# Routed attention: the mask moves into VectorE's maxima, the normalisation to GpSimd, the output copies to VectorE

## The chip, the cores and the metric

The kernel runs on one core of a Trainium2 chip. The metric is the time of one execution in microseconds on the device; the times quoted are medians of several executions. The core has five engines that run their own instruction queues and meet only at semaphores: TensorE (matmul, PE in the profile; its weight loads have their own row, PEld), VectorE (DVE), ScalarE (ACT), GpSimd (POOL) and SyncE (SP, here only for DMA issues). Matmul results land in PSUM, eight banks of 512 float32 columns by 128 partitions. VectorE and ScalarE read PSUM; GpSimd in this kernel works on SBUF only.

## What is computed

Two transformer layers over 2048 tokens of width 512. The change touches only the last block, a routed ("mixture of depths") layer: 256 of the 2048 tokens are chosen by a score, and pass through attention with 16 query heads and 8 key heads of width 128 and through a gated MLP. Its attention is

```
q = (h @ wq + bq).reshape(S, N_HEADS, HEAD_DIM)          # S = 256, 16 heads of 128
...
att = jnp.einsum('shd,thd->hst', q, kk) / np.sqrt(HEAD_DIM)
causal = jnp.tril(jnp.ones((S, S), bool))
att = jnp.where(causal[None], att, jnp.finfo(att.dtype).min)
att = jax.nn.softmax(att, axis=-1)
attn_out = jnp.einsum('hst,thd->shd', att, v).reshape(S, N_HEADS * HEAD_DIM) @ wo
```

The output of all blocks is a tensor of 1 x 2048 x 512 in float32.

## The kernel before, in words

`stage_routed` (line 2451) runs after everything else. It projects queries, keys and values (lines 2539 to 2550), does the 16 heads of attention, then the output projection (L83, called from line 2596), the norm, the gated MLP and the scatter into the output.

The 256 tokens are two tiles of 128. By causality the first tile of queries (m = 0) sees 128 keys and the second (m = 1) sees 256, so the scores of a head are 128 x 384 numbers in one PSUM bank: columns 0 to 127 for m = 0 and 128 to 383 for m = 1. Three banks (`SB`) are used in turn. For each head:

- TensorE, `scores(h)`, line 2553: for each m one float32 score matmul (L2558; in the profile each float32 matmul counts twice), and behind it a bfloat16 matmul of the identity with `G.lower` (L2560), which adds -1e30 above the diagonal into the same bank.
- VectorE, `maxima(h)`, line 2688: two reductions out of PSUM with negation (L2692), then one scaling of both results (L2696, tile `nm`).
- ScalarE, `probabilities(h)`, line 2624: two exponentials out of PSUM into the SBUF tile `pr`, with the row sums (L2629).
- VectorE, `normalised(h)`, line 2698: the reciprocals of both sums (L2700) and two multiplications of `pr` in place, 128 and 256 columns (L2703).
- TensorE, `spread(h)`, line 2564: three transposes of `pr` into PSUM (L2568). ScalarE, `spread(h)`: one copy of the 384 columns to `pt` (L2636).
- TensorE, `attend(h)`, line 2571: two products with the values (L2577, L2578). ScalarE, `output(h)`, line 2638: a copy of 128 x 256 out of PSUM to `oT` (L2640; the tile is called `bias` in the profile).

The order on each engine is written out by hand. TensorE: scores 0, scores 1, then for each h scores(h+2), spread(h), attend(h-1). VectorE: maxima 0, maxima 1, then for each h normalised(h), maxima(h+2). ScalarE: probabilities 0 and 1, then for each h spread(h), probabilities(h+2), output(h-1). GpSimd has no work in the heads: it does one multiplication for each unit of queries and keys (L2511) before them, and the scatter (L2519) at the very end. `pr`, `nm`, `ssum` and `rsum` have three buffers each, `pt` and the PSUM banks of the transposes and of the values two.

The other attention of this layer (`stage_attend1`) is not touched, but uses, on VectorE at L2134, the instruction that the change brings here, with its one-column memset (L2132), and on GpSimd an in-place select (L2036). `SB[h % 3]` is the bank of head h, and the semaphores `s_mm`, `nm_done`, `p_done`, `pn_done`, `pt_mm`, `pt_done`, `av_mm`, `o_done` count these steps in the order given.

Of the kernel before, what the change touches and what calls it, by code (L numbers as in the profile page):

```python
# [17 lines left out]
P = 128  # L18
F32 = mybir.dt.float32
F32R = mybir.dt.float32r  # L20
BF16 = mybir.dt.bfloat16
U32 = mybir.dt.uint32
I32 = mybir.dt.int32
ALU = mybir.AluOpType
ACT = mybir.ActivationFunctionType
AX = mybir.AxisListType.X
# [11 lines left out]
NEG = -1e30  # L38
# [6 lines left out]
SEL = T // 8  # L45
NS = SEL // P
NHQ, NHK, HDF = 16, 8, 128
# [469 lines left out]
def wait(eng, sem, value):  # L517

    if not isinstance(value, int) or value > 0:
        eng.wait_ge(sem, value)  # L520
# [1930 lines left out]
def stage_routed(nc, G, I, R, out):  # L2451


    names = ("qk_mm", "qb", "t1", "y", "yt_mm", "yt", "v_mm", "v", "link")
    qk_mm, qb_done, t1_done, y_done, yt_mm, yt_done, v_mm, v_done, link = (G.sem("ro_" + n) for n in names)
    b_in, hT_done = R.b_in, R.hT_done
    names = ("s_mm", "nm", "p", "pn", "pt_mm", "pt", "av_mm", "o", "wo_mm", "x1", "gu_mm", "sig", "m", "dn_mm", "delta", "gate")
    s_mm, nm_done, p_done, pn_done, pt_mm, pt_done, av_mm, o_done, wo_mm, x1_done, gu_mm, sig_done, m_done, dn_mm, delta_done, gate_done = (
        G.sem("ro_" + n) for n in names)
    wo_in, wgu_in, wd_in, added = (G.sem("ro_" + n) for n in ("wo_in", "wgu_in", "wd_in", "added"))  # L2460
    FQ, FK = NHQ * HDF, NHK * HDF
# [3 lines left out]
    scale = 1.0 / float(np.sqrt(HDF))  # L2465
    with ExitStack() as stack:
        M = Memory(nc, stack, "ro_")
# [7 lines left out]
        oT = bias[:, :].rearrange("p (h n) -> p h n", h=NHQ)  # L2475
        qT = M.sb("qT", [P, NHQ, SEL])
        kT, v = M.sb("kT", [P, NHK, SEL]), M.sb("v", [P, NS, FK])
        xs, cs, sc, hn, hT = R.xs, R.cs, R.sc, R.hn, R.hT
        x1 = M.sb("x1", [P, NS, D])
        qb, t1, y = (M.sb(n, [P, 2, BANK]) for n in ("qb", "t1", "y"))  # L2480
        nm, ssum, rsum = (M.sb(n, [P, 3, NS]) for n in ("nm", "ssum", "rsum"))
        SB = (0, 1, 6)
        pr, pt = M.sb("pr", [P, 3, 3 * P]), M.sb("pt", [P, 2, 3 * P])
        sig = M.sb("sig", [P, 2, SEL])
        gate = M.sb("gate", [P, NS])
        block = stack.enter_context(nc.Block())


# [17 lines left out]
        @block.gpsimd  # L2506
        def _(pool):
            for n, (w, off, u, m, dst) in enumerate(units):
                pool.wait_ge(qb_done, n + 1)
                wait(pool, y_done, n - 1)  # L2510
                pool.tensor_tensor(t1[:, n % 2, :].rearrange("p (h d) -> p h d", d=HDF),  # L2511
                                   qb[:, n % 2, :].rearrange("p (h d) -> p h d", d=HDF),
                                   cs[0][:, m, :].unsqueeze(1).to_broadcast([P, HB, HDF]), ALU.mult).then_inc(t1_done, 1)
            for k in range(2):
                pool.wait_ge(R.out_stored[k], 16 * NT // 2)
            for m in range(NS):
                pool.wait_ge(delta_done, m + 1)
                where = bass.IndirectOffsetOnAxis(G.idx[:, m:m + 1], 0)
                pool.indirect_dma_start(out, where, hn[:, m, :], None, compute_op=ALU.add).then_inc(added, 16)  # L2519
                pool.wait_ge(added, 16 * (m + 1))  # L2520

        @block.tensor
        def _(pe):
# [27 lines left out]


            def scores(h):
                wait(pe, p_done, NS * (h - 2))
                bank = G.ps[SB[h % 3]]
                for m in range(NS):
                    out = bank[:, m * P:(2 * m + 1) * P]
                    pe.matmul(out, qT[:, h, m * P:(m + 1) * P], kT[:, h * NHK // NHQ, 0:(m + 1) * P],  # L2558
                              start=m == 0, stop=False, skip_group_check=True)
                    last = pe.matmul(bank[:, 2 * m * P:(2 * m + 1) * P], G.identb[:, :], G.lower[:, :],  # L2560
                                     start=False, stop=True, skip_group_check=True)
                last.then_inc(s_mm, 1)

            def spread(h):
# [17 lines left out]
            pe.wait_ge(qb_done, len(units))  # L2582
            pe.wait_ge(v_done, len(vunits))
            scores(0)
            scores(1)
            for h in range(NHQ):
# [13 lines left out]
            for f in range(NF):  # L2600
                wait(pe, m_done, f - 1)
                for n, w in enumerate((wg, wu)):
                    last = mm32(pe, G.ps[2 + f % 2][:, n * SEL:(n + 1) * SEL],
                                [(w[:, c, f * P:(f + 1) * P], hT[:, c, :]) for c in range(NC)])
                last.then_inc(gu_mm, 1)
            pe.wait_ge(wd_in, 16)
            for m in range(NS):
                for f in range(NF):
                    pe.wait_ge(m_done, f + 1)
                    last = pe.matmul(G.ps[4 + m], qT[:, f, m * P:(m + 1) * P], wb[:, f, :], start=f == 0, stop=f == NF - 1)  # L2610
                last.then_inc(dn_mm, 1)

        @block.scalar
        def _(act):
            def rotated(n):
                w, off, u, m, dst = units[n]
                act.wait_ge(yt_mm, n + 1)
                act.activation(dst[:, u * HB:(u + 1) * HB, m * P:(m + 1) * P],
                               G.ps[2 + n % 2].rearrange("p (h n) -> p h n", h=HB), ACT.Copy).then_inc(yt_done, 1)

            for n in range(len(units)):
                rotated(n)

            def probabilities(h):
                for m in range(NS):
                    act.wait_ge(nm_done, NS * h + m + 1)
                    if m == 0:
                        wait(act, pt_mm, h - 2)
                    act.activation(pr[:, h % 3, m * P:(2 * m + 1) * P], G.ps[SB[h % 3]][:, m * P:(2 * m + 1) * P], ACT.Exp,  # L2629
                                   bias=nm[:, h % 3, m:m + 1], scale=scale,  # L2630
                                   accum_out=ssum[:, h % 3, m:m + 1]).then_inc(p_done, 1)

            def spread(h):
                act.wait_ge(pt_mm, h + 1)
                wait(act, av_mm, h - 1)
                act.activation(pt[:, h % 2, :], G.ps[2 + h % 2][:, 0:3 * P], ACT.Copy).then_inc(pt_done, 1)  # L2636

            def output(h):
                act.wait_ge(av_mm, h + 1)
                act.activation(oT[:, h, :], G.ps[4 + h % 2][:, 0:SEL], ACT.Copy).then_inc(o_done, 1)  # L2640

            probabilities(0)
            probabilities(1)
            for h in range(NHQ):
                spread(h)
                if h + 2 < NHQ:
                    probabilities(h + 2)
                if h >= 1:
                    output(h - 1)
            output(NHQ - 1)  # L2650
            R.root(act, 1)
            act.activation(gate[:, :], sc[:, :], ACT.Sigmoid).then_inc(gate_done, 1)
            for f in range(NF):
                act.wait_ge(gu_mm, f + 1)
                wait(act, m_done, f - 1)
                act.activation(sig[:, f % 2, :], G.ps[2 + f % 2][:, 0:SEL], ACT.Sigmoid).then_inc(sig_done, 1)

        @block.vector
        def _(dve):
            chain = Chain(dve, link)  # L2660

            dve.wait_ge(b_in[0], 16)
            for n, (w, off, u, m, dst) in enumerate(units):
                dve.wait_ge(qk_mm, n + 1)
# [10 lines left out]
                for k in range(2):  # L2675
                    last = dve.tensor_tensor(y4[:, :, k * half:(k + 1) * half], q4[:, :, (1 - k) * half:(2 - k) * half],
                                             cs[1][:, m, k * half:(k + 1) * half].unsqueeze(1).to_broadcast([P, HB, half]),
                                             ALU.mult)
# [9 lines left out]
            def maxima(h):  # L2688
                dve.wait_ge(s_mm, h + 1)
                wait(dve, p_done, NS * (h - 2))  # L2690
                for m in range(NS):
                    dve.tensor_reduce(nm[:, h % 3, m:m + 1], G.ps[SB[h % 3]][:, m * P:(2 * m + 1) * P], AX, ALU.max, negate=True  # L2692
                                      ).then_inc(link, 1)
                    chain.n += 1
                dve.wait_ge(link, chain.n)
                dve.tensor_scalar(nm[:, h % 3, :], nm[:, h % 3, :], scale, None, ALU.mult).then_inc(nm_done, NS)  # L2696

            def normalised(h):
                dve.wait_ge(p_done, NS * (h + 1))
                chain.done(dve.reciprocal(rsum[:, h % 3, :], ssum[:, h % 3, :]))  # L2700
                for m in range(NS):
                    cols = slice(m * P, (2 * m + 1) * P)
                    last = dve.tensor_scalar(pr[:, h % 3, cols], pr[:, h % 3, cols], rsum[:, h % 3, m:m + 1], None, ALU.mult)  # L2703
                last.then_inc(pn_done, 1)

            maxima(0)
            maxima(1)
            for h in range(NHQ):
                normalised(h)
                if h + 2 < NHQ:  # L2710
                    maxima(h + 2)
            for m in range(NS):
                dve.wait_ge(wo_mm, m + 1)
                dve.tensor_tensor(x1[:, m, :], G.ps[m], xs[:, m, :], ALU.add).then_inc(x1_done, 1)
# [190 lines left out]
```

## Time and profile before

| what | value |
|---|---|
| median of 3 runs | 1667.73 us (1664.67 to 1669.33) |
| the profiled execution: time, span | 1670.91 us, 1669.2 us |
| busy over the span: PE, DVE, ACT, POOL | 1549.7, 993.7, 720.6, 463.8 us |
| granted TensorE clock, mean | 0.963 of full speed (full is 2.4 GHz, the lower level 0.50, 1.2 GHz) |
| first score matmul of the routed attention | 1508.17 us |
| first matmul of its output projection | 1540.90 us |

The span runs from the first to the last instruction of the profiled execution. Busy time of TensorE contains overlaps of matmuls in the pipeline, so a busy TensorE is not one at its peak. In a timeline a row "x2" merges neighbouring instructions of the same kind; its length is from the start of the first to the end of the last. In the chain of waits the rows follow each other without overlap, so that its lengths add up.

### The profile page before, as it was taken

What the parts mean: (1) busy time and instruction counts of PE and PEld (TensorE: products, weight loads), DVE (VectorE), ACT (ScalarE), POOL (GpSimd) and SP (SyncE); (2) the same over time, 40 slices, a digit from 0 to 9 for tenths busy, and PEclk for the clock granted to TensorE, in tenths of its full rate; (3) what the DMA queues carried; (4) which work ended last, traced back from release to release, by engine and by line L of the source; (5) the groups of instructions that cost most, each with busy time, mean ns of one, the idle gap of its engine ahead of it and who ended that gap; (6) DMA issues with size and microseconds to landing.
All of it is one profiled execution on the core that took longest, in us unless ns stands there. A gap on an engine that the chain in (4) does not pass through costs nothing. (4 is left out here: it accounts for less than half of the span.)

```text
span 1669.2 us, 23334 instructions
## 1 busy us (share of the span) xinstructions
PE 1549.7 (93%) x7008; PEld 1073.0 (64%) x7008; DVE 993.7 (60%) x2739; ACT 720.6 (43%) x1218; POOL 463.8 (28%) x686
## 2 busy tenths in 40 slices
PE   5999999999999998999789999999999987899898
PEld 4877888887667776788545555555554545547484
DVE  5453666666566545877566776656677754575121
ACT  5533656565674333233234455555555541116010
POOL 0000777776432322322201121122121141130000
PEclk9999999999999999899869999999999988999899
DMA  4002222221002224467790413422431115604200
GB/s 171 1 1 82 86 88 95 78 97 58 26 26 83 95 84 127 122 187 201 218 328 19 111 35 84 112 62 56 111 66 53 62 59 166 210 29 202 101 1 13
DMA packets 100811, 158.76 MB, mean 95 GB/s; under 512 B 12004, under 2 KB 63332, under 8 KB 93160
## 3 DMA queue, kind: packets, MB, share of 16 engines
q1 hardware_dynamic: 95432, 147.34, 28.8%
q0 software_dynamic: 1920, 5.51, 1.2%
q10 hardware_dynamic: 3360, 4.72, 0.8%
q8 instruction: 46, 0.75, 0.2%
q14 instruction: 53, 0.43, 0.1%
HBM read 114.67 MB, written 42.87 MB: 94 GB/s over the span
## 5 line engine op out<-in xcount | busy, mean ns | idle before, releaser
L2064 ACT ACTIVATE l_pt<-banks 128x1024 f32<-128x1024 f32 (+3 forms) x288 | 218.5, 811 | 165.8 <-PE banks L1942 163.7
L2134 DVE CUSTOM_DVE_ANT_0 stage<-banks,l_edges 128x384 f32<-128x384 f32 (+3 forms) x384 | 201.7, 542 | 102.6 <-issue 101.6
L1979 PE MATMUL banks<-l_pt,l_v 128*64 128x512 f32 (+3 forms) x1152 | 230.6, 522 | 2.4 <-POOL l_pt L2036 2.4
L699 POOL TENSOR_TENSOR ex_hl<-ex_h,ex_hh 128x512 fp32r<-128x512 f32 x128 | 165.4, 1298 | 81.4 <-ACT ex_hh L667 81.2
L2035 POOL TENSOR_TENSOR l_turn<-l_before 128x2 f32<-128x2 f32 x192 | 39.8, 207 | 422.7 <-ACT l_pt L2064 413.1
L2137 DVE TENSOR_REDUCE l_mx<-banks 128x1 f32<-128x384 f32 (+1 forms) x208 | 113.2, 544 | 50.3 <-PE banks L1920 49.5
L732 DVE SCALAR_TENSOR_TENSOR ex_rw<-banks,ex_wb 128x512 f32<-128x512 f32 x128 | 88.3, 690 | 79.2 <-PE banks L75 79.1
L1979 PEld LDWEIGHTS banks<-l_pt,l_v 128*64 128x64 f32 x1152 | 70.3, 140 | 95.3 <-issue 71.7
L667 ACT ACTIVATE ex_hh<-ex_h 128x512 fp32r<-128x512 f32 x128 | 80.9, 632 | 103.7 <-DVE ex_h L740 102.0
L1920 PE MATMUL banks<-k,q 96*128 96x384 f32 (+3 forms) x296 | 95.1, 414 | 18.7 <-PEq L2777 8.4
L73 PE MATMUL banks<-ex_xlh,ex_wh 128*128 128x512 f32 x256 | 101.7, 397 | 2.1 <-DVE ex_rw L732 2.1
L75 PE MATMUL banks<-ex_xlh,ex_wl 128*128 128x512 f32 x256 | 99.8, 390 | 0.0
L74 PE MATMUL banks<-ex_xll,ex_wh 128*128 128x512 f32 x256 | 99.8, 390 | 0.0
L1920 PEld LDWEIGHTS banks<-k,q 96*128 96x128 f32 x296 | 54.8, 206 | 70.0 <-issue 25.0
L1920 PE MATMUL banks<-l_k,l_q 96*128 96x384 f32 (+3 forms) x296 | 88.7, 383 | 9.2 <-DVE l_mx L2134 5.5
L1920 PEld LDWEIGHTS banks<-l_k,l_q 96*128 96x128 f32 x296 | 50.2, 191 | 62.5 <-DVE l_mx L2134 26.6
L740 DVE TENSOR_TENSOR ex_h<-banks,ex_t 128x512 f32<-128x512 f32 x128 | 88.3, 690 | 1.2 <-PE banks L75 0.7
L2036 POOL TENSOR_SCALAR_AFFINE_SELECT l_pt<-l_pt 128x256 f32<-128x256 f32 x192 | 79.8, 415 | 0.1
L661 ACT ACTIVATE ex_t<-ex_rw 128x512 f32<-128x512 f32 x128 | 79.0, 617 | 1.4 <-DVE ex_rw L732 1.4
L693 POOL TENSOR_TENSOR ex_wl<-ex_ws,ex_wh 128x768 fp32r<-128x768 f32 x16 | 29.6, 1852 | 149.6 <-ACT ex_wh L655 149.6
L1942 PE MATMUL banks<-q,k 98*128 98x512 f32 (+3 forms) x288 | 69.0, 360 | 1.5 <-ACT q L2083 1.4
L1942 PE MATMUL banks<-l_q,l_k 98*128 98x512 f32 (+3 forms) x288 | 67.5, 353 | 0.5 <-ACT l_pt L2064 0.5
(405 smaller groups left out, 3384.8 us busy)
## 6 DMA issues: line engine op xcount, KB each, us to landing
ex_wb<-gates_by_expert SPq DMA_DIRECT2D x16, 1024.0 KB, 4.7
layer_v<-qkv_vs SPq DMA_DIRECT2D x16, 512.0 KB, 4.9
l_v<-layer_v SPq DMA_DIRECT2D x8, 1024.0 KB, 16.6
layer_qk<-qkv_yh SPq DMA_DIRECT2D x31, 256.0 KB, 3.2
layer_qk<-qkv_yl SPq DMA_DIRECT2D x31, 256.0 KB, 3.6
ex_ws<-ew_in SPq DMA_DIRECT2D x16, 384.0 KB, 5.0
l_q<-layer_qk SPq DMA_DIRECT2D x12, 512.0 KB, 8.0
l_k<-layer_qk SPq DMA_DIRECT2D x12, 512.0 KB, 13.7
```

Of the source, the lines that this page charges most:

```text
L73: pe.matmul(out, ah, bh, start=start and n == 0, stop=False, **kw)
L74: pe.matmul(out, ah, bl, start=False, stop=False, **kw)
L75: last = pe.matmul(out, al, bh, start=False, stop=stop and end, **kw)
L699: pool.tensor_tensor(hl[:, k % RING, :], h[:, k % RING, :], raw(hh[:, k % RING, :]), ALU.subtract).then_inc(hl_done, 1)
L732: dve.scalar_tensor_tensor(rw[:, k % 2, :], gate[k % 2][:, :], 0.0, wb[:, par, b * TB:(b + 1) * TB], ALU.max, ALU.mult).then_inc(rw_done, 1)
L740: dve.tensor_tensor(h[:, k % RING, :], up[k % 2][:, :], tt[:, k % 2, :], ALU.mult).then_inc(h_done, 1)
L1920: pe.matmul(out, q[par][0:K3, h, qt * P:(qt + 1) * P], k[par][0:K3, h, k0 * P:k1 * P], start=True, stop=True).then_inc(a_mm, 1)
L1942: last = pe.matmul(bank[:, 0:width], k[par][0:KM, h, kt * P:(kt + 1) * P], q[par][0:KM, h, qa * P:(qz + 1) * P], start=True, stop=True)
L1979: last = pe.matmul(bank[h * 2 * HD:(h + 1) * 2 * HD, (qa - b * BT) * P:(qz + 1 - b * BT) * P], v[par][:, kt, h, :], pt[:, step_part(b, j), ...
L2064: act.activation(pt[:, step_part(b, j), :, 0:width], G.banks[:, 2 * slot:2 * slot + 2, 0:width], ACT.Exp, scale=scale).then_inc(p_done, 1)
L2134: dve.tensor_tensor_reduce(cutoff[:, n % 4, 0:width], G.ps[5 + n % MB][:, 0:width], masked, 1.0, NEG, ALU.add, ALU.max, mx[:, h, m, c:c + ...
L2137: dve.reduce_max(mx[:, h, m, c:c + 1], G.ps[5 + n % MB][:, 0:width], axis=AX).then_inc(a_red, 1)
```

## The change

Four edits, all in `stage_routed`. The bfloat16 mask matmuls go; VectorE adds a wide mask tile (zeros, then the causal triangle) and takes the maxima in one instruction, `tensor_tensor_reduce`, that writes the masked scores to `pr` in SBUF. ScalarE's exponential then works in place on `pr`, no longer out of PSUM. The two multiplications with the reciprocal sums go from VectorE to GpSimd, with a new semaphore `rsum`. The output copies go from ScalarE to VectorE, two heads late: `output(h - 2)` stands after `maxima(h + 2)` and so before `inverses(h + 1)`. The scores of head h wait for the maxima of head h-3 where they had waited for its exponentials, and the maxima of head h wait for the transposes of head h-3.

```diff
+        wide = M.sb("wide", [P, 2 * P], BF16)
+        carry = M.sb("carry", [P, 4, 1])
...
@@ gpsimd
+            for h in range(NHQ):
+                pool.wait_ge(rsum_done, h + 1)
+                for m in range(NS):
+                    cols = slice(m * P, (2 * m + 1) * P)
+                    last = pool.tensor_scalar(pr[:, h % 3, cols], pr[:, h % 3, cols], rsum[:, h % 3, m:m + 1], None, ALU.mult)
+                last.then_inc(pn_done, 1)
@@ tensor, scores(h)
-                wait(pe, p_done, NS * (h - 2))
+                wait(pe, nm_done, NS * (h - 2))
...
-                    out = bank[:, m * P:(2 * m + 1) * P]
-                    pe.matmul(out, qT[:, h, m * P:(m + 1) * P], kT[:, h * NHK // NHQ, 0:(m + 1) * P],
-                              start=m == 0, stop=False, skip_group_check=True)
-                    last = pe.matmul(bank[:, 2 * m * P:(2 * m + 1) * P], G.identb[:, :], G.lower[:, :],
-                                     start=False, stop=True, skip_group_check=True)
+                    last = pe.matmul(bank[:, m * P:(2 * m + 1) * P], qT[:, h, m * P:(m + 1) * P],
+                                     kT[:, h * NHK // NHQ, 0:(m + 1) * P], start=m == 0, stop=m == NS - 1,
+                                     skip_group_check=True)
@@ scalar, probabilities(h)
-                    if m == 0:
-                        wait(act, pt_mm, h - 2)
-                    act.activation(pr[:, h % 3, m * P:(2 * m + 1) * P], G.ps[SB[h % 3]][:, m * P:(2 * m + 1) * P], ACT.Exp,
+                    cols = slice(m * P, (2 * m + 1) * P)
+                    act.activation(pr[:, h % 3, cols], pr[:, h % 3, cols], ACT.Exp,
@@ scalar
-            def output(h):
-                act.wait_ge(av_mm, h + 1)
-                act.activation(oT[:, h, :], G.ps[4 + h % 2][:, 0:SEL], ACT.Copy).then_inc(o_done, 1)
...
-                if h >= 1:
-                    output(h - 1)
-            output(NHQ - 1)
@@ vector, at the start of the stage
+            dve.memset(wide[:, 0:P], 0.0)
+            chain.done(dve.tensor_copy(wide[:, P:2 * P], G.lower[:, :]))
@@ vector, maxima(h)
+                wait(dve, pt_mm, h - 2)
                 for m in range(NS):
-                    dve.tensor_reduce(nm[:, h % 3, m:m + 1], G.ps[SB[h % 3]][:, m * P:(2 * m + 1) * P], AX, ALU.max, negate=True
-                                      ).then_inc(link, 1)
+                    cols = slice(m * P, (2 * m + 1) * P)
+                    dve.memset(carry[:, 2 * (h % 2) + m, :], 0.0)
+                    dve.tensor_tensor_reduce(pr[:, h % 3, cols], G.ps[SB[h % 3]][:, cols], wide[:, (1 - m) * P:2 * P],
+                                             1.0, NEG, ALU.add, ALU.max, nm[:, h % 3, m:m + 1]).then_inc(link, 1)
...
-                dve.tensor_scalar(nm[:, h % 3, :], nm[:, h % 3, :], scale, None, ALU.mult).then_inc(nm_done, NS)
-
-            def normalised(h):
+                dve.tensor_scalar(nm[:, h % 3, :], nm[:, h % 3, :], -scale, None, ALU.mult).then_inc(nm_done, NS)
+
+            def inverses(h):
                 dve.wait_ge(p_done, NS * (h + 1))
-                chain.done(dve.reciprocal(rsum[:, h % 3, :], ssum[:, h % 3, :]))
-                for m in range(NS):
-                    cols = slice(m * P, (2 * m + 1) * P)
-                    last = dve.tensor_scalar(pr[:, h % 3, cols], pr[:, h % 3, cols], rsum[:, h % 3, m:m + 1], None, ALU.mult)
-                last.then_inc(pn_done, 1)
+                dve.reciprocal(rsum[:, h % 3, :], ssum[:, h % 3, :]).then_inc(rsum_done, 1)
+
+            def output(h):
+                dve.wait_ge(av_mm, h + 1)
+                dve.tensor_copy(oT[:, h, :], G.ps[4 + h % 2][:, 0:SEL]).then_inc(o_done, 1)
 
             maxima(0)
             maxima(1)
             for h in range(NHQ):
-                normalised(h)
+                inverses(h)
                 if h + 2 < NHQ:
                     maxima(h + 2)
+                if h >= 2:
+                    output(h - 2)
+            output(NHQ - 2)
+            output(NHQ - 1)
```

## Rows read from the trace of the kernel before

**Rows 1.** Busy time of each engine in the middle of the stage; then granted clock, DMA.

```profile
core 0: us, PE busy (x) PEld busy (x) DVE busy (x) ACT busy (x) POOL busy (x), PEclk, DMA share, GB/s
1514.60:1535.60 21.00, 21.00 (x152) 18.29 (x151) 15.77 (x68) 19.08 (x71) 0.00 (x0) 1.00 0.70 290
```

**Rows 2.** Chain of waits in order of time: start, length, engine, tile, line.

```profile
1508.17 0.46 PE banks L2558 x2
...
1518.27 0.22 PE banks L2558 x2
...
1518.55 0.49 PE banks L2558 x2
...
1519.09 0.34 PE banks L2568 x3
1519.43 0.43 PE banks L2577 x2
1519.86 0.22 PE banks L2578 x2
...
1540.90 27.72 PE banks L83 x64
```

**Rows 3.** Timeline of one head: start, length, engine, line, operation, tiles.

```profile
1519.92 0.39 PE L2558 MATMUL banks<-ro_kT,ro_qT 128*128 128x128 f32 x2
...
1520.94 0.62 DVE L2692 TENSOR_REDUCE ro_nm<-banks 128x1 f32<-128x128 f32 x2 [0.26 <-PE banks L2560]
...
1521.67 0.17 DVE L2696 TENSOR_SCALAR ro_nm<-ro_nm 128x2 f32<-128x2 f32 x1
1521.75 0.16 DVE L2700 RECIPROCAL ro_rsum<-ro_ssum 128x2 f32<-128x2 f32 x1
...
1521.94 0.55 DVE L2703 TENSOR_SCALAR ro_pr<-ro_pr,ro_rsum 128x128 f32<-128x128 f32 x2
...
1522.60 0.50 PE L2568 MATMUL banks<-ident,ro_pr 128*128 128x128 f32 x3
```

**Rows 4.** Timeline, TensorE: the transposes of heads 0, 1, 14 and 15.

```profile
1511.95 0.55 PE L2568 MATMUL banks<-ident,ro_pr 128*128 128x128 f32 x3 [0.97 <-DVE ro_pr L2703]
...
1513.40 0.55 PE L2568 MATMUL banks<-ident,ro_pr 128*128 128x128 f32 x3
...
1537.21 0.55 PE L2568 MATMUL banks<-ident,ro_pr 128*128 128x128 f32 x3 [0.61 <-DVE ro_pr L2703]
...
1538.29 0.55 PE L2568 MATMUL banks<-ident,ro_pr 128*128 128x128 f32 x3
```

**Rows 5.** VectorE: two timeline rows; groups by shape, busy us, mean ns, idle.

```profile
899.65 0.42 DVE L2134 CUSTOM_DVE_ANT_0 stage<-banks,l_edges 128x256 f32<-128x256 f32 x1 [1.19 <-issue]
...
900.11 0.17 DVE L2145 TENSOR_REDUCE l_nm<-l_mx 128x8 f32<-128x16 f32 x1
...
L2134 DVE CUSTOM_DVE_ANT_0 stage<-banks,l_edges 128x128 f32<-128x128 f32 x16 | 4.6, 285 | 2.0 <-issue 2.0
...
L2720 DVE TENSOR_TENSOR ro_sig<-banks,ro_sig 128x256 f32<-128x256 f32 x16 | 6.8, 425 | 45.7 <-ACT ro_sig L2656 45.7
...
L2703 DVE TENSOR_SCALAR ro_pr<-ro_pr,ro_rsum 128x256 f32<-128x256 f32 x16 | 5.6, 347 | 0.0
```

**Rows 6.** Timeline: a GpSimd instruction that waits for the VectorE instruction.

```profile
1453.75 0.69 DVE L2669 TENSOR_TENSOR ro_qb<-banks,bias 128x512 f32<-128x512 f32 x1
...
1454.52 1.51 POOL L2511 TENSOR_TENSOR ro_t<-ro_qb,routed_cos 128x512 f32<-128x512 f32 x1 [1.85 <-DVE ro_qb L2669]
```

**Rows 7.** GpSimd's groups by shape, over the whole span.

```profile
L699 POOL TENSOR_TENSOR ex_hl<-ex_h,ex_hh 128x512 fp32r<-128x512 f32 x128 | 165.4, 1298 | 81.4 <-ACT ex_hh L667 81.2
L2036 POOL TENSOR_SCALAR_AFFINE_SELECT l_pt<-l_pt 128x256 f32<-128x256 f32 x192 | 79.8, 415 | 0.1
...
L118 POOL TENSOR_SCALAR_AFFINE_SELECT ident<-ident 128x128 f32<-128x128 f32 x1 | 0.3, 285 | 0.2 <-POOL lower L116 0.2
```

**Rows 8.** Busy time by stretch again, of two others with TensorE partly idle.

```profile
1336.00:1346.00 10.00, 6.93 (x37) 3.41 (x35) 9.32 (x23) 3.89 (x7) 4.35 (x6) 1.00 0.00 0
...
1573.00:1581.00 8.00, 7.15 (x20) 5.76 (x21) 1.79 (x4) 0.80 (x2) 0.00 (x0) 0.50 1.04 392
```

More of the change, by code:

```diff
@@ L2456, in stage_routed @@
     b_in, hT_done = R.b_in, R.hT_done
-    names = ("s_mm", "nm", "p", "pn", "pt_mm", "pt", "av_mm", "o", "wo_mm", "x1", "gu_mm", "sig", "m", "dn_mm", "delta", "gate")
-    s_mm, nm_done, p_done, pn_done, pt_mm, pt_done, av_mm, o_done, wo_mm, x1_done, gu_mm, sig_done, m_done, dn_mm, delta_done, gate_done = (
+    names = ("s_mm", "nm", "p", "pn", "pt_mm", "pt", "av_mm", "o", "wo_mm", "x1", "gu_mm", "sig", "m", "dn_mm", "delta", "gate", "rsum")
+    s_mm, nm_done, p_done, pn_done, pt_mm, pt_done, av_mm, o_done, wo_mm, x1_done, gu_mm, sig_done, m_done, dn_mm, delta_done, gate_done, rsum_done = (
         G.sem("ro_" + n) for n in names)
```

## Prediction

> **What bounds the kernel now.** I looked first at the busy shares by stretch, to see whether the changed stage has one full engine. In the 21.00 us in the middle of the routed attention the matmul engine is busy all the time, ScalarE 19.08 us and VectorE 15.77 us; GpSimd has nothing there [rows 1]. By that view the stage is TensorE's, and the two matmuls taken out per head look like pure gain. The chain of waits, read next, gives TensorE's pieces for one head: scores 0.22, then 0.06 up to the next row for the first mask matmul, scores 0.49, 0.05 up to the transposes for the second mask matmul, three transposes 0.34, then 0.43 and 0.22 for the two products with the values, 1.81 in all [rows 2]. The stage runs from 1508.17 to 1540.90, 32.73 us [rows 2].
>
> The timeline shows a second bound that the busy share hides [rows 3]. The program order of VectorE is: normalise head h, maxima of head h+2, normalise head h+1. TensorE's order is: scores h+2, transposes h, values h-1, scores h+3, transposes h+1. So a loop runs through both engines. From the first score matmul of head h+2 (1519.92) to its first maximum is 1.02 us; 0.73 to the scaling; 0.08 to the reciprocal of head h+1; 0.19 to its normalisation; 0.55 for that pair, over at 1522.49. The transposes of head h+1 start at 1522.60, 0.11 later. Of that I take 0.05 for the wake-up. TensorE then does those transposes (0.38 when they were waited for) and values h (0.65) before it comes to scores h+4. The loop covers two heads: 1.02 + 0.73 + 0.08 + 0.19 + 0.55 + 0.05 + 0.38 + 0.65 = 3.65 us, 1.83 per head. The trace has 13 head periods between the transposes of 1513.40 and 1537.21: 23.81 us, 1.832 each [rows 4]. So TensorE and this loop bound the stage together, and the question is what the change does to the loop.
>
> **The change, step by step.**
>
> 1. Mask matmuls out. 32 go, two per head. TensorE loses their two pieces, 0.06 and 0.05 [rows 2], and the second score piece should shrink from 0.49 to the 0.43 that the same 256 columns take with the values [rows 2]: 0.17 per head. Bounds: 0.11 if only the mask pieces go, 0.17 if the other does too. I take 0.17, since the two 256-column products have the same work. TensorE alone would need 1.64 to 1.65 per head. The same 0.17 comes off the first term of the loop: 1.02 becomes 0.85.
>
> 2. Maxima with the mask. The new instruction is in the trace, in the other attention: 0.285 us for 128 columns and 0.42 for 256, and 0.46 from the start of the latter to the next instruction that needs its result (899.65 to 900.11), accumulator read included [rows 5]. The instructions overlap by 0.07, so the 128-column one adds 0.22: 0.68 until the scaling starts, against 0.73 now. The memset of one column ahead of each could add up to 0.06 each; I take nothing, since the instruction itself must wait for the matmuls and the first memset precedes only the first of them. Bounds 0.62 to 0.80.
>
> 3. The outputs come to VectorE. A copy of 128x256 out of PSUM now stands, in program order, between the scaling of head h+2 and the reciprocal of head h+1, so all of it is in the loop. A plain copy out of PSUM of that size isn't in the trace of this stage; a two-operand VectorE instruction over the same PSUM shape takes 0.425 [rows 5], less 0.07 of overlap 0.35. The bounds are 0.28 (the SBUF normalisation of the same shape, 0.347 [rows 5], less 0.07) and 0.42 (no overlap). On ScalarE the output copy goes away, but ScalarE is not in the loop. Its rest per head, two exponentials and the spread, was already finished in time; the gain there is nothing in the steady part. The data of these outputs was ready a head earlier (head h-2), so there is no wait for them.
>
> 4. Normalisation on GpSimd. The 0.19 from the reciprocal to the normalisation becomes a hand-over to another engine: from the end of a VectorE instruction (1453.75 + 0.69) to a GpSimd start is 0.08 [rows 6]; with the 0.16 of the reciprocal [rows 3] that is 0.24. For the work itself there is no GpSimd multiply by a scalar in the trace. The nearest rows are its one-input selects in place: 0.415 for 128x256 and 0.285 for 128x128 [rows 7], 0.70 for the pair. From above: a two-input GpSimd instruction takes 1.298 for 512 columns [rows 7], so by columns 0.65 + 0.32 = 0.97, and with a fixed start in each up to 1.13. From below: not under VectorE's own 0.55 [rows 3]. I take 0.70, because those are one-input, in place, float32, and of the same two shapes.
>
> The Trainium skill, "GPSIMD Engine Reference", section 8 (Key points), says that for elementwise work VectorE is structurally about twice as fast. The trace agrees for two inputs (1.298 on GpSimd [rows 7] against 0.69 on VectorE [rows 6], both 512 columns); for one input it does not (0.415 against VectorE's 0.347, 256 columns [rows 7, 5]), and section 4.1 of the page (Engine selection) itself calls one-input work roughly line-rate. By the first rule the time is that of rival A.
>
> 5. The rest. The score matmuls now wait for the maxima instead of the exponentials, which is earlier, and the maxima wait for transposes of a head that TensorE finished one period before; neither ends last. The one-time fill of the wide mask tile stands on VectorE before its first bias addition, which must wait for TensorE's first four 512-column matmuls anyway; nothing. The exponentials read SBUF in place of PSUM; off the loop.
>
> New loop for two heads: 0.85 + 0.68 + 0.08 + 0.35 + 0.24 + 0.70 + 0.05 + 0.38 + 0.65 = 3.98 us, 1.99 per head against 1.832. TensorE would now stand idle 0.34 of each period and wait for GpSimd at the transposes. 13 periods at +0.16 are +2.1 us.
>
> The ends go the other way. To the first head's transposes it is 3.78 now (1508.17 to 1511.95 [rows 2, 4]); of its terms the scores lose 0.17 and the maxima 0.05, the hand-over gains 0.05 and the normalisation 0.15: 3.76, -0.02. From there to the second head's it is 1.45 now; its probabilities will be ready, and TensorE has only the first head's transposes and the scores of head 3 in between, 0.35 and 0.65, 1.00: -0.45. The last two sets lie 1.08 apart now [rows 4], and become 0.38 + 0.65 = 1.03: -0.05. From the last set to the output projection it is 2.61 (1538.29 to 1540.90 [rows 2, 4]); the copy that ends it moves between engines at about its length, and the spread before it no longer queues behind an output copy on ScalarE, worth 0 to 0.2; I take 0. Together -0.5.
>
> Sum: 2.1 - 0.5 = **+1.6 us**, 0.1%. The profiled execution took 1670.91 us (span 1669.2), so its like would take 1672.5; it lies 3.2 above the median of the three runs, 1667.73, and on that median the forecast is **1669.3 us**.
>
> What a different price is worth: 0.1 us on the loop costs 0.05 per head, 0.65 over 13 periods, and with the first head and the fill about 0.15 more: 8 us for each us on the loop.
>
> **The rivals.**
>
> A. GpSimd is at half of VectorE's speed here too (the other side: slower). Place: the two GpSimd multiplications of each head, on the loop. VectorE's pair is 0.347 + 0.27 = 0.62 without its overlap [rows 3, 5], so 1.24. 0.54 more at 8 gives +4.3, so +5.9: 1673.6. It decides, with more than 5 us, from a pair of about 1.13. For it: the two-input row. Against it: the select rows [rows 7]. The rule of "GPSIMD Engine Reference" in the Trainium skill, told above, speaks for it.
>
> B. The clock falls. TensorE's idle share in the stage goes from nothing to some 17%. For it: after the wait near 1568 the granted clock was 0.50 for 8 us at 7.15 busy [rows 8]. Against it: 10 us at 6.93 busy kept 1.00 [rows 8]. At the lower level a head takes TensorE 3.3 instead of 1.99, so one stretch of 8 us serves 2.4 heads and not 4.0, 1.6 heads or about 3.2 us more, with the 1.6 of the forecast: 1672.5.
>
> C. The loop doesn't bind (faster). If the handover hides and TensorE sets the pace at 1.65, 13 periods give -2.4 and the ends -0.5: -2.9, 1664.8. For it: TensorE's busy share. Against it: with no output copy at all and everything else as above the loop is still 3.63, 1.82 per head; the GpSimd pair would have to take less than 0.38 for any gain in the steady part, which is below every bound of step 4.
>
> **How the numbers follow.** Forecast 0.60, A 0.19, B 0.11, C 0.10. A change within 0.3% (5 us) is what a measurement of this kernel can't tell from none. The forecast's own range, from the bounds of steps 1 to 4 (0.55 to 1.05 for the GpSimd pair, 0.1 either way for the others together), is -0.4 to +5. Faster by more: 0.01 from the forecast, 0.03 from C, 0.04. Slower by more: 0.04 from the forecast, 0.14 from A, 0.05 from B, 0.23. Same: 0.73. The range goes down to 1665.5, between C and the forecast, and up to 1674.3, just past A.
>
> **What would show it.** Head period, from one set of transposes to the next: 1.99; 1.65 shows C, 2.26 shows A, over 3 with the clock at 0.50 shows B. TensorE's wait ahead of the transposes should be put down to GpSimd, about 0.35 per head. VectorE: first maximum to scaling 0.68, output copy 0.42, right before each reciprocal. GpSimd: 16 pairs of 0.70. Scores: the 256-column piece 0.43. The forecast is wrong if the GpSimd pair is outside 0.5 to 1.1, or if TensorE waits for something else than GpSimd.

## The result: 9.4 us slower, where 1.6 was forecast

| | before | after |
|---|---|---|
| median of 14 runs each | 1666.62 us (1661.23 to 1670.43) | 1676.06 us (1669.63 to 1680.36) |
| ratio | | 1.006, 95% interval 1.0046 to 1.0074 |
| profiled execution: time, span | 1670.91, 1669.2 | 1676.22, 1674.5 |
| first score matmul to output projection | 1508.17 to 1540.90, 32.73 us | 1502.80 to 1546.89, 44.09 us |
| head period (between transposes) | 1.832 | 2.44, and 2.476 over the 13 of [rows 4] |

The stage, from the first score matmul of the routed attention to the output projection, got 11.4 us longer. The two profiled executions differ by 5.4 us the other way before the stage begins, in code that the change hardly touches. I take that as run to run: over all the kernels of this document, which share that code, the stage begins anywhere from 1499.81 to 1508.17. So the stage is what to compare, and its 11.4 lies inside the interval of the whole (7.7 to 12.3 us).

The busy times by stretch, in the same columns as [rows 1]: TensorE, full before, has 21.42 of 29.00 us; GpSimd has 17.79. Nothing looks full any more.

```profile
1512.00:1541.00 29.00, 21.42 (x129) 16.45 (x128) 14.55 (x108) 16.10 (x57) 17.79 (x25) 1.00 0.41 169
```

The timeline of the changed kernel, around one lap of the loop (two heads), answers [rows 3]:

```profile
1525.22 0.55 PE L2574 MATMUL banks<-ident,ro_pr 128*128 128x128 f32 x3 [1.23 <-POOL ro_pr L2520]
...
1526.26 0.82 PE L2565 MATMUL banks<-ro_kT,ro_qT 128*128 128x128 f32 x4
...
1527.13 0.29 DVE L2695 CUSTOM_DVE_ANT_0 ro_pr<-banks,ro_wide 128x128 f32<-128x128 f32 x1 [1.77 <-ACT ro_pr L2634]
...
1527.88 0.17 DVE L2699 TENSOR_SCALAR ro_nm<-ro_nm 128x2 f32<-128x2 f32 x1
...
1527.96 0.42 DVE L2707 COPY bias<-banks 128x256 f32<-128x256 f32 x1
...
1528.29 0.15 DVE L2703 RECIPROCAL ro_rsum<-ro_ssum 128x2 f32<-128x2 f32 x1
...
1528.54 1.51 POOL L2520 TENSOR_SCALAR ro_pr<-ro_pr,ro_rsum 128x128 f32<-128x128 f32 x2 [1.58 <-DVE ro_rsum L2703]
...
1530.10 0.55 PE L2574 MATMUL banks<-ident,ro_pr 128*128 128x128 f32 x3 [1.23 <-POOL ro_pr L2520]
```

Read the starts: scores to first maximum 0.87, to the scaling 0.75, to the output copy 0.08, to the reciprocal 0.33, to GpSimd 0.25, and then **1.56 to the transposes**. TensorE needs 1.04 from transposes to scores (1525.22 to 1526.26, at the start of the lap). 0.87 + 0.75 + 0.08 + 0.33 + 0.25 + 1.56 + 1.04 = 4.88 us for two heads, 2.44 each. The profile names ScalarE as releaser of the first maximum, but the exponentials that this maximum waits for belong to the head three before it and had ended over 4 us earlier. It starts 0.05 after the end of the score matmuls (1526.26 + 0.82), and the same 0.87 from their start stands in the laps before and after. GpSimd's groups in the changed kernel, in the columns of [rows 7] but from 1508 us on, so with 15 of the 16 heads:

```profile
L2520 POOL TENSOR_SCALAR ro_pr<-ro_pr,ro_rsum 128x256 f32<-128x256 f32 x15 | 13.9, 925 | 0.0
...
L2520 POOL TENSOR_SCALAR ro_pr<-ro_pr,ro_rsum 128x128 f32<-128x128 f32 x15 | 9.1, 605 | 13.5 <-DVE ro_rsum L2703 13.5
```

The rest is for the most part the clock. The third column from the end (PEclk) shows the granted clock at both ends of the stage below full speed; within these stretches, from 1508 to 1511 and from 1542 to 1545, it is 0.50:

```profile
1506.00:1509.00 3.00, 1.42 (x6) 1.38 (x7) 0.70 (x7) 1.13 (x5) 3.00 (x4) 0.79 1.02 434
1509.00:1512.00 3.00, 3.00 (x13) 2.25 (x11) 0.88 (x8) 2.16 (x9) 1.20 (x3) 0.65 1.01 429
...
1541.00:1544.00 3.00, 2.41 (x10) 1.91 (x10) 0.85 (x3) 1.30 (x5) 2.11 (x3) 0.64 0.00 0
1544.00:1547.00 3.00, 2.39 (x12) 2.00 (x11) 1.01 (x3) 1.77 (x2) 0.00 (x0) 0.79 0.00 0
```

### The profile page after: what moved, and what is told of

It reads as the page before. It is cut to its first block and busy times, and to the rows that moved or that the text cites. A ratio compares the mean times of both kernels' runs of the same rounds, so it can differ in the third digit from the quotient of the medians.

```text
span 1674.5 us, 23323 instructions
## 1 busy us (share of the span) xinstructions
PE 1547.2 (92%) x6976; PEld 1070.2 (64%) x6976; DVE 991.4 (59%) x2789; ACT 717.0 (43%) x1202; POOL 488.5 (29%) x718
```

## The experiments

All edits are against the changed kernel unless said otherwise. "Period" is read from the starts of the transposes in the middle of the stage, "stage" from the first score matmul to the output projection, in the profiled execution. The ratio is to the kernel before on the same chip. "GpSimd pair" is the length of GpSimd's two multiplications of one head, from the start of the first to the end of the second; in e12 there is only one. In the expected texts, theory S says that the loop's sum is right and only this pair was mis-sized; rival O says that the order of work on VectorE cost the time.

| run | GpSimd pair | loop sum expected | period | stage | ratio (95%) |
|---|---|---|---|---|---|
| before | none | 1.83 | 1.83 | 32.73 | |
| changed | 1.51 | (1.99) | 2.44 | 44.09 | 1.006 (1.0046 to 1.0074) |
| e1 normalisation on VectorE | none | 1.93 | 1.93 | 35.68 | 1.0008 (0.9993 to 1.0023) |
| e2 GpSimd alone, on before | 1.50 | 2.33 | 2.34 | 42.35 | 1.0044 (1.0028 to 1.0061) |
| e3 mask alone | none | 1.76 | 1.77 | 31.85 | 0.9997 (0.9981 to 1.0014) |
| e4 output copy out of the loop | 1.50 | 2.27 | 2.27 | 41.90 | 1.0059 (1.0038 to 1.008) |
| e5 constant | 1.34 | 2.04 or 2.4 | 2.35 | 42.14 | one run |
| e6 broadcast operand | 0.97 | 2.2 to 2.3 | 2.16 | 39.06 | one run |
| e8 filler | 1.50 | 2.44 | 2.44 | 42.30 | 1.0059 (1.0034 to 1.0085) |
| e10 scores ahead | 1.50 | 1.86 to 1.95 | 1.90 | 36.89 | 1.0046 (1.003 to 1.0063) |
| e12 split | 0.76 | 1.98 | 2.07 | 35.83 | one run |
| e9 mask, scores ahead | none | 1.70 | 1.64 | 30.17 | 0.9987 (0.9971 to 1.0003) |
| e11 scores ahead, broadcast | 0.97 | 1.65 to 1.75 | 1.64 | 31.60 | 0.9997 (0.9982 to 1.0011) |

**e1, normalisation back on VectorE.** In `inverses(h)` the two `dve.tensor_scalar` of before; GpSimd's loop goes.

```diff
-                dve.reciprocal(rsum[:, h % 3, :], ssum[:, h % 3, :]).then_inc(rsum_done, 1)
+                chain.done(dve.reciprocal(rsum[:, h % 3, :], ssum[:, h % 3, :]))
+                for m in range(NS):
+                    cols = slice(m * P, (2 * m + 1) * P)
+                    last = dve.tensor_scalar(pr[:, h % 3, cols], pr[:, h % 3, cols], rsum[:, h % 3, m:m + 1], None, ALU.mult)
+                last.then_inc(pn_done, 1)
```

> The changed kernel with one part undone: the two multiplications by the reciprocal sums are VectorE's again. Theory S (size of one term): the loop over two heads that the prediction added up is right, and only the GpSimd pair was mis-sized (1.51 us in the changed kernel's trace, 0.70 in the sum). Then the loop here is 0.87 + 0.75 + 0.08 + 0.33 + 0.19 + 0.55 + 0.05 + 1.04 = 3.86, head period 1.93 us; the stage from first score matmul to output projection takes 33 to 34 us against 32.73 before and 44.09 with the whole change, the clock stays at 1.00 in it, and the time is that of before within 0.1%. Rival O (order): the output copy and the masked maxima in VectorE's program order cost most. Then the head period stays above 2.2 and the time at least 5 us above before.

Period 1.93, as summed. The stage took 35.68, longer than the 33 to 34 expected: the clock did fall here, at 1507 to 1512 (0.66 in the mean), against what was expected. The whole time can't be told from that of before. VectorE's new work and order cost 0.10 of the 0.61 us per head (1.93 against 1.83), so they are not the main cause.

**e2, GpSimd alone.** The kernel before, with only its `dve.tensor_scalar` pair replaced by the new GpSimd loop.

> The kernel before with one part of the change: GpSimd does the two multiplications, all else as before. Theory S: loop 1.02 + 0.73 + 0.08 + 0.24 + 1.51 + 0.05 + 1.03 = 4.66, head period 2.33 us, stage 41 to 44 us (+8 to +11), the upper end with the TensorE clock at 0.50 for a few us at the stage's ends. Rival O: head period below 2.0, stage under 36 us.

2.34 per head (1525.77 to 1535.12 are four), stage 42.35: this edit alone gives 9.6 of the 11.4 us.

**e3, mask alone.** e1's edit, and the output copies back on ScalarE.

> The changed kernel with two parts undone: normalisation on VectorE and output copies on ScalarE as before; only the mask stands in VectorE's maxima. Theory S: loop 0.87 + 0.75 + 0.08 + 0.19 + 0.55 + 0.05 + 1.03 = 3.52, head period 1.76 against 1.832, stage 31.5 (-1.2 us). Rival O would have this at or above the time before: the masked maxima cost VectorE more than the mask matmuls cost TensorE, head period 1.83 or more.

1.77 (1521.53 to 1528.60), stage 0.9 shorter; the times can't tell it from before.

**e4, order on VectorE.**

```diff
                 inverses(h)
+                if h >= 3:
+                    output(h - 3)
                 if h + 2 < NHQ:
                     maxima(h + 2)
-                if h >= 2:
-                    output(h - 2)
+            output(NHQ - 3)
             output(NHQ - 2)
```

> The changed kernel with only the order on VectorE changed: the output copy stands after the reciprocal of the next head and one head later (output h-3 behind inverses h), so it is out of the loop. Theory S: 4.88 less 0.33 to 0.35 is 4.54, head period 2.27 against 2.44 (both 13 periods with the rest), the stage 2.2 us shorter than the changed kernel's 44.09. Rival O expects the period to fall to 2.0 or less. If GpSimd itself were the bound (1.51 a head), nothing would move.

2.27, and the stage 2.2 shorter. The output copy cost what step 3 said.

**e5 and e6, what makes GpSimd slow.** e5 puts the constant `1.0 / P` where `rsum[:, h % 3, m:m + 1]` stood (it leaves the normalisation out). e6:

```diff
-                    last = pool.tensor_scalar(pr[:, h % 3, cols], pr[:, h % 3, cols], rsum[:, h % 3, m:m + 1], None, ALU.mult)
+                    last = pool.tensor_tensor(pr[:, h % 3, cols], pr[:, h % 3, cols],
+                                              rsum[:, h % 3, m:m + 1].to_broadcast([P, (m + 1) * P]), ALU.mult)
```

> The changed kernel, but GpSimd multiplies by the constant 1/128 and not by the reciprocal sums (the normalisation is left out, same instruction, same columns, same waits). If the per-partition scalar operand is what makes the instruction slow, the pair falls from 1.51 us to near the 0.70 of the selects, and by the loop sum (4.88 less 0.8) the head period from 2.44 to about 2.04. If the multiplication itself is slow on GpSimd, the pair stays at 1.4 to 1.5 us and the period at 2.4.

> The changed kernel, but GpSimd's multiplication takes the reciprocal sum as a second tensor operand, broadcast along the columns, and not as a per-partition scalar. By the two-input rows (1.298 us for 512 columns, 1.5 with a broadcast) the pair takes 1.0 to 1.2 us, 0.3 to 0.5 less than now, and the head period falls to 2.2 to 2.3. If the cost goes by columns whatever the operands, the pair stays at 1.5.

GpSimd's groups in e5, then in e6:

```profile
L2520 POOL TENSOR_SCALAR ro_pr<-ro_pr 128x256 f32<-128x256 f32 x16 | 13.5, 846 | 0.0
L2520 POOL TENSOR_SCALAR ro_pr<-ro_pr 128x128 f32<-128x128 f32 x16 | 8.5, 529 | 31.1 <-DVE ro_rsum L2703 31.1
```

```profile
L2520 POOL TENSOR_TENSOR ro_pr<-ro_pr,ro_rsum 128x256 f32<-128x256 f32 x16 | 9.8, 612 | 0.0
L2520 POOL TENSOR_TENSOR ro_pr<-ro_pr,ro_rsum 128x128 f32<-128x128 f32 x16 | 6.4, 399 | 34.0 <-DVE ro_rsum L2704 34.0
```

The scalar operand costs only 0.08 per instruction (605 to 529, 925 to 846). The one-input instruction itself goes at (846 - 529) / 128 = 2.5 ns per column; the same product written with a second, broadcast tensor at (612 - 399) / 128 = 1.7, and is a third shorter. The periods followed the pair: 1.34 and 0.97 in place of 1.51 in the sum give 2.36 and 2.17, and 2.35 and 2.16 were measured.

**e8, filler.** TensorE gets work that nobody reads.

```diff
+                for _ in range(40 if h == 0 else 8):
+                    pe.matmul(G.ps[7][:, 0:P], G.identb[:, :], G.lower[:, :], start=True, stop=True, skip_group_check=True)
                 spread(h)
```

> The changed kernel with extra TensorE work that nobody reads (128-column bfloat16 matmuls into the unused bank 7: 40 ahead of the first head's transposes, 8 ahead of each other head's). It fills TensorE's idle time with work and lies within it. If the low granted clock in the stage's first and last heads (0.50 for about 4 us each in the changed kernel) comes from TensorE's idling and costs what the sum leaves over (44.09 less what 2.44 a head gives), the clock stays at 1.00 and the stage takes 41.5 to 42.5 us. If the clock has no part in it, the stage stays at 44 or gets longer.

The busy times of e8 by stretch, in the columns of [rows 1]. The clock is 1.00 throughout:

```profile
1506.00:1509.00 3.00, 2.67 (x37) 2.35 (x35) 0.97 (x9) 1.40 (x6) 2.73 (x4) 1.00 1.00 426
1509.00:1512.00 3.00, 2.89 (x30) 2.52 (x28) 1.54 (x15) 2.16 (x9) 1.78 (x3) 1.00 1.02 431
...
1543.00:1546.00 3.00, 2.39 (x13) 1.77 (x12) 0.85 (x2) 1.77 (x2) 0.00 (x0) 1.00 0.00 0
```

The stage is 1.8 us shorter at the same period, 42.30 against 44.09, and the difference lies where the changed kernel's clock was low: 0.4 between heads 0 and 1, 0.5 in the 13 periods of [rows 4], 0.3 between heads 14 and 15, 0.6 from there to the output projection. That is the clock's share. The whole time doesn't resolve it (1.0059 against 1.006).

**e10, scores three heads ahead.** Possible since the maxima now free the bank.

```diff
             scores(1)
+            scores(2)
             for h in range(NHQ):
-                if h + 2 < NHQ:
-                    scores(h + 2)
+                if h + 3 < NHQ:
+                    scores(h + 3)
```

> The changed kernel with only TensorE's order changed: scores run three heads ahead and not two, which the change allows since the maxima free the PSUM bank. It leaves GpSimd's 1.51 us and VectorE's order alone. Theory S: the loop no longer holds the score matmuls. What is left over two heads are: transposes to ScalarE 0.58, spread 0.39, exponentials to reciprocal 0.94, hand-over 0.24, GpSimd 1.51, 0.05, in all 3.7, 1.86 per head; and transposes, maxima 0.75, 0.08, output 0.33, 0.24, 1.51, 0.05 with 0.55 is 3.5. Head period 1.86 to 1.95 against 2.44, stage 35 to 38 us. If GpSimd's slowness by itself (not its place in the loop) cost the time, the period stays at 2.4.

1.90 (1520.38 to 1527.97 are four) with GpSimd as slow as ever: 0.54 us per head went by moving its 1.5 us out of the loop with the scores, without making them shorter. The whole time is still above before, by 0.3 to 0.6% (5.0 to 10.5 us); the stage is 4.2 us above.

**e12, split.** GpSimd multiplies columns 0 to 127, VectorE the other 256 after its reciprocal, each with a semaphore of its own.

> The changed kernel with the GpSimd term halved: GpSimd multiplies only the 128 columns of the first tile, VectorE the 256 of the second, at the same time. Theory S: the loop's GpSimd term falls from 1.51 to 0.60, so 0.87 + 0.75 + 0.08 + 0.33 + 0.24 + 0.60 + 0.05 + 1.04 = 3.96, head period 1.98. A cost that goes with the hand-over between engines, not with the length of GpSimd's work, would leave the period above 2.3.

2.07 (1517.52 to 1525.79), 0.09 above the sum. The reason is in the groups of e12: beside VectorE's multiplication GpSimd's instruction takes 762 ns, and not 605. On the loop that is 0.16 for two heads, 0.08 per head.

```profile
L2518 POOL TENSOR_SCALAR ro_pr<-ro_pr,ro_rsum 128x128 f32<-128x128 f32 x16 | 12.2, 762 | 34.1 <-DVE ro_rsum L2701 34.1
...
L2703 DVE TENSOR_SCALAR ro_pr<-ro_pr,ro_rsum 128x256 f32<-128x256 f32 x16 | 5.7, 353 | 0.6
```

**e9 and e11, two versions.** e9 is e3 with e10's edit, e11 is the changed kernel with e6's and e10's.

> A version against both: the mask in VectorE's maxima, normalisation on VectorE and output copies on ScalarE as before, and TensorE's scores three heads ahead. Theory S: the loop without the score matmuls is below each engine's own work; TensorE has 1.64 per head, ScalarE 0.88 + 0.39 + 0.40 = about 1.70, VectorE 1.5. Head period 1.70 against 1.832, stage 30.5 to 31 (about -2 us, 0.1%), which the times can hardly tell from before. If a loop through both engines still bound it, the period would stay at the 1.76 of the kernel without the third head ahead.

> The whole change with two repairs: scores three heads ahead, and GpSimd's multiplication with the reciprocal sums as a broadcast tensor operand (1.01 us a pair, measured). Theory S: the loop through ScalarE is 0.58 + 0.39 + 0.94 + 0.24 + 1.01 + 0.05 = 3.2, 1.60 per head, below TensorE's 1.64; head period 1.65 to 1.75; stage 32 to 34 us with the low clock at its start. So the change with all its parts would stand within 1 us of before. If GpSimd's part can't be hidden, the period stays at 1.9 or more.

Both run at 1.64, the sum of TensorE's own pieces. Transposes four heads apart, from the timelines of e9 and of e11:

```profile
1523.02 0.49 PE L2568 MATMUL banks<-ident,ro_pr 128*128 128x128 f32 x3
...
1529.58 0.49 PE L2568 MATMUL banks<-ident,ro_pr 128*128 128x128 f32 x3
```

```profile
1519.23 0.49 PE L2575 MATMUL banks<-ident,ro_pr 128*128 128x128 f32 x3
...
1525.79 0.49 PE L2575 MATMUL banks<-ident,ro_pr 128*128 128x128 f32 x3
```

So the whole change, with two repairs, is back at the time of before, and e9 shortens the stage by 2.6 us; its ratio, 0.9987, is not clear of 1. ScalarE's 1.70, which was to bound e9, was too high a sum. But it is full there too: from 1517 to 1530 TensorE is busy 13.00 of 13.00 us and ScalarE 12.94, and the chain of waits in that stretch runs through ScalarE alone, 1.64 per head. In e11, where VectorE has the output copies, ScalarE is busy 10.79 of the same 13.00.

## Why the prediction was wrong

The forecast was +1.6 us. The range from the forecast's own bounds ended at +5 and the whole range at 1674.3, +6.6 on the median it was stated on; +9.4 was measured. The mechanism was right, TensorE waiting at the transposes for GpSimd in a loop over two heads, and one term of it was far off.

- **Step 4 failed**: "I take 0.70, because those are one-input, in place, float32, and of the same two shapes." The pair takes 1.51. Even the upper bound, 1.13, and rival A's 1.24 were below it (the fixed start inside the 1.13 has no row of its own). An in-place select and a multiplication by a scalar share shape and type but not their cost per column (1.0 ns between its two shapes against 2.5). Bounding from above by the two-input row assumed that one input is never slower than two; e6 shows that it can be.
- **What the miss in the stage is made of.** It is 9.8 us. With the clock held up (e8) 8.0 of them are left: 5.8 in the 13 periods (31.7 against 25.9), 1.0 before the first transposes (4.77 against 3.76), 0.5 and 0.7 between heads 0 and 1 and between heads 14 and 15, where the pair stands alone and I had put TensorE's 1.00 and 1.03; they took 1.49 and 1.70 (in the changed kernel, with the low clock, 1.89 and 2.00). My rule of 8 us for each us on the loop gives only 6.5 for the 0.81 that the pair was too short, so it was low, chiefly for these ends. The other 1.8 are the clock.
- **The rest of the loop held.** Terms summed 0.85, 0.68, 0.08, 0.35, 0.24; measured 0.87, 0.75, 0.08, 0.33, 0.25. With the terms as measured in the changed kernel the same sum gave the period of e1 to e4 within 0.01, before they ran. TensorE waited for GpSimd 1.23 us in every second head, where I had 0.35 in each. The masked maxima were 0.07 dearer: 0.52 to 0.53 from the second one's start to the scaling (1527.35 to 1527.88), not 0.46.
- **Step 1 held**: e3 has the mask edit alone, at 1.77 where the sum said 1.76. Step 3 too (e4).
- **Rival A** had the place right (TensorE waits for GpSimd at the transposes) and its price too low. The Trainium skill, "GPSIMD Engine Reference", section 8 (Key points), says VectorE is about twice as fast for elementwise work; here it is 2.1 to 2.7 times (605 on GpSimd against 286 ns on VectorE in the kernel before, 925 against 347). The remark in its section 4.1 (Engine selection) that one input is roughly line-rate, which I let speak against the rule, doesn't hold for this instruction.
- **Rival B** came true in part. It wasn't the busy share in the middle of the stage, which kept 1.00 at 21.42 of 29.00, but the waits at its two ends. It came on top of the forecast's mechanism, not in its place: 1.8 us by e8. The same fall in e1 cost its stage some 1.7 us (26.8 in its 13 periods, where 13 times 1.93 is 25.1).
- **Rival C** fell: in the changed kernel the loop binds, at 2.44, and TensorE's own 1.64 never shows. With the mask edit alone the loop still binds (e3, 1.77). e9 and e11, which take the scores out of it, do reach 1.64.
- The ranges were too narrow because the one term without a row of its own was bounded by rows of other operations, and its factor of 8 makes each 0.1 us nearly 1 us.

One thing stays open: the stage got 11.4 us longer in one profiled execution, the median time 9.4. I take the rest as scatter, since the interval covers it, but no run was made for it. Each stage length here comes from a single execution, and in e10 the two don't fit so well: 4.2 us in the stage, 5.0 to 10.5 in the time.

## What to carry to other kernels

When a stage has a full engine, still sum the loop that goes through two engines' program orders: here it equalled the full engine's time, and every instruction moved between its links cost half its length per head. Moving work to an idle engine puts its latency into such a loop; before that, let the producer run one step further ahead (here one line, once the bank is freed early). And an instruction that no row shows has no upper bound from its neighbours: time it first, or let the range reach to more than twice its nearest row (here 1.51 against 0.70).

## What the hardware showed that was not expected

- GpSimd multiplies float32 by a per-partition scalar at 605 ns for 128 columns and 925 for 256, by a constant at 529 and 846, and by a broadcast tensor at 399 and 612. So the form with a second tensor, here one column broadcast, is faster than the one-input form; a full second tensor was not run at these shapes.
- GpSimd and VectorE slow each other. GpSimd's 605 became 762 beside a 353 ns VectorE multiplication out of SBUF (e12). In the changed kernel VectorE's scaling of two columns took 0.40 at 1524.79, while GpSimd multiplied, and 0.17 at 1527.88, while it didn't; in e10, from 1520 to 1530, where GpSimd is at work each time, it took 0.31 to 0.39. VectorE's next instruction followed 0.08 after the start of the scaling in either case of the changed kernel, so this cost the loop nothing there. The Trainium skill, "GPSIMD Engine Reference", section 8 (Key points), says that the two share their SBUF interfaces, with contention where the VectorE instruction is in a 2-port perf mode or has two SBUF inputs. The trace agrees that they slow each other; in which mode VectorE ran, no row here shows.
- TensorE's clock fell to 0.50 for 3 to 4 us after the wait of the first head (2.58 us ahead of its transposes), in the changed kernel, e1, e2, e4, e5, e6 and e10, and not in before, e3, e9, e11 and e12. Those also wait there, by 0.86 to 1.81 us, and e1 fell after 1.51, so the length of that wait alone doesn't tell, and what does stays open. With the wait filled (e8) it stayed at 1.00.
